# Selective scan on Trainium2: scan partitions regrouped from 128 channels to 8 channels x 16 states

## What is computed

```python
def step(h, inp):
    dt_t, B_t, C_t, u_t = inp
    dA = jnp.exp(dt_t[..., None] * A)
    dBu = (dt_t * u_t)[..., None] * B_t[:, None, :]
    h = dA * h + dBu
    y = jnp.einsum('bdn,bn->bd', h, C_t)
    return (h, y)
...
dt = jax.nn.softplus(jnp.einsum('blr,dr->bld', dt_lo, dt_w) + dt_b)
A = -jnp.exp(A_log)
y = _selective_scan(dt, Bm, Cm, xc, A, Dp)
y = y * jax.nn.silu(z)
```

## Time and profile before

| | |
|---|---|
| median of 3 runs | 5928.38 us (5915.49 to 5931.79) |
| the profiled execution: time, span | 5918.2 us, 5916.4 us |
| busy: PE, DVE, ACT | 81%, 89%, 58% |
| first scan starts, last scan starts | 66.0 us, 5722.6 us |
| mean granted TensorE clock | 0.883 of 2.4 GHz |
| DMA issues: b_rows and c_rows 256, bc_rows 64, patches 32, text 32, output 32, weights 14 | 430 |

### The profile page before, as it was taken

One profiled execution on the slowest core, in us unless ns is written; L12 is line 12 of the kernel. 1 busy time (PEld: TensorE's weight loads), 2 busy tenths in 40 slices (PEclk: granted clock), 3 DMA queues, 4 the chain that ended last, 5 costly groups with the idle time before them and its releaser, 6 DMA issues.

```text
span 5916.4 us, 67241 instructions
## 1 busy us (share of the span) xinstructions
PE 4785.9 (81%) x22624; PEld 3257.5 (55%) x22624; DVE 5259.6 (89%) x4154; ACT 3457.5 (58%) x7266; POOL 1.5 (0%) x9
## 2 busy tenths in 40 slices
PE   5788878877878787888788888888888888888877
PEld 3555555555555555555555555555555655555554
DVE  6999998989999898998999999898998989989971
ACT  3455655555565555665556666566565656656643
POOL 0000000000000000000000000000000000000000
PEclk8888988888889888888889999998999989989985
DMA  3112211212112112112112111112112112111110
GB/s 105 59 44 67 66 41 60 68 38 67 58 43 68 61 45 68 55 47 66 60 45 67 63 45 60 61 45 66 54 47 68 45 60 66 41 61 60 41 32 2
DMA packets 56890, 327.57 MB, mean 55 GB/s; under 512 B 13245, under 2 KB 15741, under 8 KB 23626
## 3 DMA queue, kind: packets, MB, share of 16 engines
q1 hardware_dynamic: 56490, 322.53, 17.3%
HBM read 313.52 MB, written 8.98 MB: 55 GB/s over the span
## 4 chain that ended last, share of the span: by engine, by line
DVE 42%; PE 37%; issue 16%; ACT 4%; DVEq 1%; DMA 0%; SPq 0%; ACTq 0%; POOL 0%; POOLq 0%
DVE hs L993 15%; PE y_ps L426 9%; DVE hs L997 7%; DVE hs L976 5%; PE f_ps L549 4%; DVE neg_max L1100 3%; PE f_ps L597 3%; PE f_ps L505 3%; DVE xc L1056 3%; PE f_ps L522 3%; PE f_ps L608 3%; PE f_ps L496 2%; PE a_ps L474 2%; PE f_ps L562 2%; PE a_ps L464 2%
## 5 line engine op out<-in xcount | busy, mean ns | idle before, releaser
L993 DVE TENSOR_TENSOR_SCAN hs<-decay,hs 128x2192 f32<-128x2192 f32 x384 | 1812.3, 4719 | 19.5 <-DVE decay L983 2.2
L426 PE MATMUL y_ps<-hs,ident 128*128 128x274 f32 x5376 | 1612.7, 433 | 81.9 <-DVE hs L1001 29.5
L736 ACT ACTIVATE decay<-dt,inner_s 128x273 f32<-128x273 f32 x3072 | 1384.7, 517 | 98.7 <-issue 53.1
L426 PEld LDWEIGHTS y_ps<-hs,ident 128*128 128x128 f32 x5376 | 1082.4, 208 | 445.5 <-issue 148.7
L976 DVE TENSOR_TENSOR hs<-b_rows,dtu 128x2192 f32<-128x2192 f32 x384 | 935.6, 2436 | 90.7 <-PE y_ps L426 67.7
L997 DVE TENSOR_TENSOR hs<-hs,c_rows 128x2192 f32<-128x2192 f32 x384 | 935.0, 2435 | 4.5
L549 PE MATMUL f_ps<-ident,hid 92*92 92x92 f32 x3456 | 481.8, 283 | 507.3 <-ACT hid L820 507.3
L549 PEld LDWEIGHTS f_ps<-ident,hid 92*92 92x92 f32 x3456 | 340.9, 141 | 694.1 <-ACT hid L820 616.3
L820 ACT ACTIVATE hid<-f_ps,neg_max 92x274 f32<-92x274 f32 x1152 | 463.3, 481 | 341.3 <-DVE neg_max L1100 341.1
L464 PE MATMUL a_ps<-xn,w_in_s 96*128 96x274 f32 x1536 | 472.9, 435 | 8.9 <-ACT xi L759 5.4
L1100 DVE TENSOR_REDUCE neg_max<-f_ps 92x4 f32<-92x1096 f32 x288 | 370.4, 1286 | 92.2 <-PE f_ps L542 92.0
(11 more groups left out here) (114 smaller groups left out, 5115.3 us busy)
## 6 DMA issues: line engine op xcount, KB each, us to landing
b_rows<-bc_rows SPq DMA_DIRECT2D x128, 1096.0 KB, 5.6
c_rows<-bc_rows SPq DMA_DIRECT2D x128, 1096.0 KB, 5.6
xp<-in_patches SPq DMA_DIRECT2D x32, 588.0 KB, 7.4
out<-h SPq DMA_DIRECT2D x32, 205.5 KB, 2.2
bc_rows<-bc_s SPq DMA_DIRECT2D x64, 34.2 KB, 1.5
h<-in_txt SPq DMA_DIRECT2D x32, 57.8 KB, 2.3
w_in_s<-in_w_in SPq DMA_DIRECT2D x1, 1152.0 KB
fc_s<-in_fc SPq DMA_DIRECT2D x2, 576.0 KB
```

The costliest lines, as they stand in the source:

```text
L426: mm = pe.matmul(y_ps[:, 0:T], ident[:, :], hs[q % 2][:, n, :], start=(q % 2 == 0 and n == 0), stop=(q % 2 == 1 and n == end - 1))
L736: e = act.activation(decay[half][:, n, t], dt[d][:, u, t], ACT.Exp, scale=inner_s[:, d, u, s:s + 1])
L993: dve.tensor_tensor_scan(i, a, i, 0.0, ALU.mult, ALU.add).then_inc(scan_done, 1)
```

## The change

The scan's partitions become 8 channels x 16 states, and its eight free tiles hold 64 channels, so a unit is again two scans of 128 x 2192.

- dt and dtu (dt * u) are written by channel to device memory (write_rows, 12 writes an element) and read back with each channel's row repeated for its 16 states, dt into decay and dtu into hs (read_half, 24 reads an element of 1.1 MB each). decay has three buffers, hs four. ACT takes the exponential in place. dt and dtu have one buffer each for both directions.
- B and C are one tile each for a direction. A matmul with a selection matrix spreads the 16 rows over the 128 partitions: B stays in PSUM (b_ps), C is copied to SBUF (c_s). spread_rows and its loads are gone.
- The state sum is eight matmuls a scan with 32 output columns each (y_pick), in four column groups; the paired additions are gone.
- a_ps is one bank, as b_ps takes the other: each matmul of the front waits for the copy of the one before.
- The softplus runs by chunk. Its max(x, 0) moves from DVE to ACT (Relu), and the zeroing of the edges too, now for every scan.
- x_proj and the step sizes move by one gap, and the output product, the scan and the next input product stand in the order of gaps 0, 1, 2. A set-up builds the selection matrices and A's columns once.

```diff
+        b_ps = ctx.enter_context(nc.psum_tensor("b_ps", [128, 512], F32))
+        a_ps = ctx.enter_context(nc.psum_tensor("a_ps", [128, 512], F32))
...
+        dt_rows = nc.dram_tensor("dt_rows", (2, IC, 32, 4, T), F32, kind="Internal").ap()
+        def row_of_channels(rows, d, u):
+            return rows[d, u].rearrange("r a t -> a r t")
+
+        def half_unit(rows, q):
+            halves = rows[q // 6, (q // 2) % IC].rearrange("(e h b) a t -> e h (b a t)", h=2, b=2)
+            return halves[:, q % 2, :].unsqueeze(1).broadcast_to([EDD, N, TILES * T])
...
+            def write_rows(b, d, u):
+                before = anew(ago(b, 1), SCANS, 6 * d + 2 * u + 2, 40 * b[1] + 30 + 3 * d + u)
+                sp.wait_ge(dt_ready, at(b, 6, 3 * d + u + 1))
+                wait(sp, exp_done, before)
+                sp.dma_start(row_of_channels(dt_rows, d, u), dt[:, u, :]).then_inc(dt_stored[u], 16)
+                sp.wait_ge(dtu_ready, at(b, 6, 3 * d + u + 1))
+                wait(sp, dbu_done, before)
+                sp.dma_start(row_of_channels(dtu_rows, d, u), dtu[:, u, :]).then_inc(dtu_stored[u], 16)
+
+            def read_half(b, q):
+                d, u = q // 6, (q // 2) % IC
+                sp.wait_ge(dt_stored[u], at(b, 32, 16 * (d + 1)))
+                wait(sp, scan_done, anew(b, SCANS, q - 2, 40 * b[1] + 2 * q + 1))
+                sp.dma_start(decay[q % 3][:, :, :], half_unit(dt_rows, q)).then_inc(dt_in[q % 3], 16)
+                sp.wait_ge(dtu_stored[u], at(b, 32, 16 * (d + 1)))
+                wait(sp, ysum, anew(b, SCANS, q - 3, 40 * b[1] + 2 * q + 2))
+                sp.dma_start(hs[q % 4][:, :, :], half_unit(dtu_rows, q)).then_inc(dtu_in[q % 4], 16)
+
+            def first_rows(b):
+                write_rows(b, 0, 0)
+                read_half(b, 0)
+                write_rows(b, 0, 1)
+                read_half(b, 1)
+                write_rows(b, 0, 2)
...
             def step(b, f, e, a):
                 if a is not None:
                     load_patches(a)
+                read_half(b, 2)
+                read_half(b, 3)
+                read_half(b, 4)
                 if e is not None:
                     store(e[0])
                 if a is not None:
                     load_txt(a)
-                spread_rows(b, 1)
+                read_half(b, 5)
+                write_rows(b, 1, 0)
+                read_half(b, 6)
+                write_rows(b, 1, 1)
+                read_half(b, 7)
+                write_rows(b, 1, 2)
+                for q in range(8, SCANS):
+                    read_half(b, q)
                 if a is not None:
-                    spread_rows(a, 0)
+                    first_rows(a)
...
+            def sum_states(b, q):
+                wait(pe, hc_done, at(b, SCANS, q + 1))
+                if q % 2 == 0:
+                    wait(pe, gate_tmp, at(b, UNITS, q // 2))
+                for v in range(2):
+                    for g in range(4):
+                        mm = pe.matmul(y_ps[32 * g:32 * g + 32, 0:T], y_pick[:, 2 * (q % 2) + v, :],
+                                       hs[q % 4][:, 4 * v + g, :], start=(q % 2 == 0 and v == 0),
+                                       stop=(q % 2 == 1 and v == 1), skip_group_check=True)
+                mm.then_inc(ysum, 1)
...
             def in_proj(b, d, lo, hi):
                 if lo == 0:
                     pe.wait_ge(xn_ready, at(b, 1, 1))
+                    wait(pe, c_copied, at(b, 2, d))
                 for j in range(lo, hi):
+                    if j >= 1:
+                        pe.wait_ge(xz_copied, at(b, 12, 6 * d + j))
...
+            def c_spread(b, d):
+                pe.wait_ge(dtv_abs, at(b, 6, 3 * d + 3))
+                pe.wait_ge(dtv_relu, at(b, 6, 3 * d + 3))
+                pe.matmul(a_ps[:, 0:T], spread[32:32 + 2 * N, 1, :], dt_lo[32:32 + 2 * N, :],
+                          start=True, stop=True).then_inc(c_mm, 1)
+
+            def b_spread(b, d):
+                pe.wait_ge(dtlo_ready, at(b, 2, d + 1))
+                wait(pe, dbu_done, at(b, SCANS, 6 * d))
+                pe.matmul(b_ps[:, 0:T], spread[32:32 + 2 * N, 0, :], dt_lo[32:32 + 2 * N, :],
+                          start=True, stop=True).then_inc(b_mm, 1)
...
             def exps(b, q, lo, hi):
...
+                    act.wait_ge(dt_in[q % 3], at(b, 64, 16 * (q // 3) + 16))
+                    t = 0 if d == 0 else T - 1
+                    act.activation(dec[:, :, t:t + 1], zero_c[:, 0:1].unsqueeze(1).broadcast_to([128, TILES, 1]),
+                                   ACT.Copy).then_inc(edge, 1)
+                for k in range(lo, hi):
+                    t = slice(1, T) if d == 0 else slice(0, T - 1)
+                    e = act.activation(dec[:, k, t], dec[:, k, t], ACT.Exp,
+                                       scale=a_cols[:, d * IC + u, TILES * half + k:TILES * half + k + 1])
...
+            def dt_parts(b, d, j):
                 act.wait_ge(dtv_mm, at(b, 6, 3 * d + j + 1))
+                wait(act, dtu_stored[j], at(b, 32, 16 * d))
+                act.activation(dtu[:, j, :], a_ps[:, 0:T], ACT.Abs).then_inc(dtv_abs, 1)
+                wait(act, dt_stored[j], at(b, 32, 16 * d))
+                act.activation(dt[:, j, :], a_ps[:, 0:T], ACT.Relu).then_inc(dtv_relu, 1)
+                act.wait_ge(dtv_abs, at(b, 6, 3 * d + j + 1))
+                act.activation(dtu[:, j, :], dtu[:, j, :], ACT.Exp, scale=-1.0).then_inc(sp_exp, 1)
+                act.wait_ge(sp_exp, at(b, 6, 3 * d + j + 1))
+                act.activation(dtu[:, j, :], dtu[:, j, :], ACT.Ln, bias=one_c[:, 0:1]).then_inc(sp_ln, 1)
...
+            def input_product(b, q):
+                d, x = q // 6, hs[q % 4]
+                dve.wait_ge(dtu_in[q % 4], at(b, 48, 16 * (q // 4) + 16))
+                dve.wait_ge(b_mm, at(b, 2, d + 1))
+                dve.tensor_tensor(x[:, :, :], x[:, :, :], b_ps[:, 0:T].unsqueeze(1).broadcast_to([128, TILES, T]),
+                                  ALU.mult).then_inc(dbu_done, 1)
...
+            def output_product(b, q):
+                d, x = q // 6, hs[q % 4]
+                dve.wait_ge(scan_done, at(b, SCANS, q + 1))
+                dve.wait_ge(c_copied, at(b, 2, d + 1))
+                dve.tensor_tensor(x[:, :, :], x[:, :, :], c_s[d][:, :].unsqueeze(1).broadcast_to([128, TILES, T]),
+                                  ALU.mult).then_inc(hc_done, 1)
```

More of the change, by code:

```diff
@@ L666, in fronts_early @@
                 x, xd = (b, 1) if d == 0 else (a, 0)
-                if x is not None and gap == 9:
+                if x is not None and gap == XP_GAP:
                     x_proj_mm(x, xd)
@@ L670, in fronts_early @@
                     dt_mm(x, xd, DT_GAPS.index(gap))
+                if x is not None and gap == C_GAP:
+                    c_spread(x, xd)
+                if x is not None and gap == B_GAP:
+                    b_spread(x, xd)
                 if d == 0 and a is not None:
@@ L702, in front @@
                 b = (0, 0)
+                for u in range(UNITS):
+                    pe.wait_ge(s_l, u + 1)
+                    mm = pe.matmul(f_ps[:, 0, COLS * u:COLS * (u + 1)], a_spread(u), col_mask,
+                                   start=True, stop=True)
+                mm.then_inc(s_lm, 1)
                 tok(b, (0, 1))
@@ L715, in finish @@
                         fine_late(*e, 2 * GAPS + gap)
[L716 to L718 removed]
+                    if gap == 1:
+                        sum_states(f[0], SCANS - 1)
                     fine_early(*f, gap)
@@ L947, in front @@
                 for j in range(IC):
-                    dt_abs(b, 0, j)
-                for part in range(2):
-                    softplus(b, 0, part)
-                act.wait_ge(a_neg, 1)
-                exps(b, 0, 0, NH)
+                    dt_parts(b, 0, j)
+                c_copy(b, 0)
+                act.wait_ge(s_ac, 1)
+                exps(b, 0, 0, TILES)
             def finish(f, e):
```

308 lines of the change are left out of this document (140 added, 168 removed).

## The result

The kernel after the change took 7365.3 us, the median of its runs (7301.9 to 7392.1), against 5930.1 (5915.5 to 5944.3) for the kernel before on the same chip: a ratio of 1.241, 95% interval 1.238 to 1.244. It is slower by 1435 us. The prediction said 5725 and a range of 5550 to 6250. The profiled execution took 7392.1 us, its span is 7390.3.

What follows compares the result with a forecast made beforehand. It took DVE's work plus its waits on PE and ACT as the bound. 5918.2 - 195 - 140 + 30 + 80 (transfers) + 20 = 5713 us, stated as 5725 by the median of runs; range 5550 to 6250.

Steps and rivals of the forecast that it cites:

- R: Time of one read of dt or dtu from device memory, taken as 5.6 us on 8 engines.
- The rival: Rival 1: transfers become the bound, deciding from 5.8 us a read, slower from 6.1; priced at 6050 us, chance 0.24.
- that formula: Transfer-bound time: 24 R + 12 x 2.3 + 3 us an element, times 31.9, plus 86 and 194 us.
- rivals 3 and 4: Reads spread over 16 engines, 5645 us, chance 0.09; state sum's column groups don't run side by side, 5865, chance 0.03.
- DVE's own work, -195: Halving adds, step-size maxima and edge memsets leave DVE, 215.7 us; softplus by chunk adds 20.5; net -195.
- The state sum, -140: On PE, 16 short passes a scan, 0.7 us instead of 3.1, save 140 of DVE's 180.6 us of waits.
- ACT's added work, +190 and hidden: Edge copies, Relu, split Exp and Ln add about 190 us, hidden in ACT's 42% free time except where DVE waits.
- One bank, +30: Front's matmuls share one PSUM bank, PE waits for ACT's copies, delaying row maxima and MLP's sums; +30 us.
- rival 2: PE's chains lengthen: clock and bank double the 256.7 us of waits; 5950 us, clock near 0.7, chance 0.12.
- the three waits of 256.7 us: DVE's waits on chains of PE and ACT: rstd 105.4, row maxima 92.0, MLP's sums 59.3 us.
- The front, +20: Before the first scan: one write, one read and 12 copies and parts in series; +20 us, 10 to 35.
- the prediction for sixteen engines: Rival 3: reads spread over 16 engines, the 80 us for transfers go; 5645 us, chance 0.09.

Runs made afterwards that it cites:

- e3: Changed kernel with reads on 16 engines, two buffers for the output tile h2 and each write of rows split in four: 5938.7 us, ratio 1.001.
- e7: e6 with the state sum as eight full-width identity matmuls a scan instead of column groups (output not the reference's): 6114.4 us, ratio 1.031.
- e6: e3 with two PSUM banks for the front again and B copied to SBUF by ACT: 5947.6 us, ratio 1.003.
- e9: e3 without ACT's clearing copies at the edge and its Relu (output incomplete): 6042.3 us, ratio 1.020.
- e5: Kernel before the change with only the front's single PSUM bank and the one-gap shift of x_proj and step sizes: 5989.8 us, ratio 1.010.
- e12: e3 with ACT copying chunk 0 of the input projection in gap 0, ahead of the gelus: 5840.4 us, ratio 0.984.
- e1: Changed kernel with the repeat of the states outermost in the reads' source, so reads get 16 engines: 6111.0 us, ratio 1.030.
- e8: e3 with each read bringing one tile of eight, 140 KB instead of 1.12 MB (data left out): 5891.5 us, ratio 0.996.

## Why the prediction was wrong

**The step that failed** is the length of a read, R. It was right that a read gets 8 engines: 9437 completion packets of 4 bytes stand in the trace after, which is 768 reads x 8, 384 writes x 4, 96 loads and stores of the elements x 16, 13 weights x 16, and 12 and 1 for the two parts of the step-size weights. It was wrong to take 5.6 us from "At the slow start 16 engines fetch the same 8.8 KB at 237 GB/s; eight engines, each on a row of its own, ask for only 212". That sentence holds device memory to be the only thing that engines share. They also share the way into SBUF. Alone, a read takes 9.7 to 10.2 us; inside the kernel the packets average 469 ns, 7.5 us a read, close to the 0.445 us and 7.1 that the prediction had worked out as the mean of the kernel before and set aside. The rival's point of decision, 5.8 us, was computed rightly, the 0.2 us of margin should have been read as no knowledge at all, and the rival's own sum said 6690 for R = 7.1; pricing it at 6050 and ending the range at 6250 cut off what the argument had produced. R = 7.5 in that formula gives (24 x 7.5 + 30.6) x 31.9 + 280 = 6998 us. The kernel without the store's wait took 6965; its own packets average 450 ns, R = 7.2, and the formula gives 6768, so it is good to some 200 us and its hit with 7.5 is luck. (The chances have a slip too: those of the forecast and rivals 3 and 4 sum to 0.64, and with "a little of 2" to more than the 0.63 given for faster.)

**The store.** The prediction asked for each moved or added transfer what stands behind it, and didn't ask it for the transfers that were there. A store issued behind reads in the same queue landed after 20.2 us instead of 2.2, with DVE waiting: 400 us in the kernel after, 129 with the reads on sixteen engines.

**DVE's own work, -195:** right. -200.9 in the kernel after (5259.6 to 5058.7), the input product from PSUM at 2429 ns.

**The state sum, -140:** right in kind, too low in size. The waits of 180.6 us went to 3.6 in the kernel after and to 30.7 in e3; full-width sums cost 167 us (e7 against e6). Sixteen passes load in 0.62 us at full clock, where 0.7 was said.

**ACT's added work, +190 and hidden:** right. The groups add up to 189 us (edge copies 81.5, Relu 75.3, splits 13.3 and 18.9), ACT's busy time rises only by 94.4, since neighbouring instructions overlap (their durations sum to 174 us more, the time with any of them running is 94 us more), and e9's undisturbed large elements are no shorter without 157 us of it.

**One bank, +30:** the mechanism was right, the size wrong, and of the two victims named the second, the MLP's sums, was hit in the changed kernel. In the kernel before it costs 57 us (e5) and hits a third, the state sum; in the changed one it costs at least 98, the part that e12 gives back. The prediction looked for slack ahead of the waits on average ("slack of two gaps lies ahead of most of them") and not for the one gap where ACT has 7 us of other work before its copy.

**Clock:** the granted mean fell from 0.883 to 0.724 of 2.4 GHz, near the 0.7 of rival 2, whose waits of over 400 us on PE and ACT are there too. They are in good part transfers' waits passed on: row maxima fall from 405.0 to 240.5 us in e1 and 225.3 in e3. But with the transfers mended rival 2 is nearly there: the three waits of 256.7 us, which the term of +30 let grow little and the rival let double, are 594.1 us in e3 and 471.4 in e12, +215. What the clock of 0.79 itself costs isn't isolated; e7 shows that more work on PE isn't the cure.

**The front, +20:** the first scan starts at 99.6 us instead of 66.0, +34, within the bounds of 10 to 35.

**What stays open.** e12 is at 5840, the prediction for sixteen engines was 5645. Of these 195 us the stalls at the loop's edge and the waits for rows come to some 33 to 47 by e8, the later first scan is some 25 (90.6 us against 66.0) and was told at 20. The rest is in the waits for row maxima (219.9 against 92.0), the MLP's product (116.0 against 59.3), rstd (135.5 against 105.4) and o_s (102.3 against 41.2), chains through PE and ACT at a lower clock and in another order of gaps; the runs don't split these.

## What to carry to other kernels

Before a transfer is given a rate, count its engines and then look at which partitions they write at the same moment; where the engines' blocks met, up to half the rate was lost, and a small load-only kernel showed it. Weigh it against the number of engines: the form that mended this kernel has the same slow packets on twice as many. When traffic triples, list every transfer that already shares the queue and who waits for it, not only the new ones. When a buffer goes from two to one, search the order of the engine that empties it for its longest piece of other work, and put the emptying first.

## What the hardware did that I had not expected

- With nothing else running, packets of 8768 bytes take mostly 331 ns or about 660, which fits whether another engine writes 32 partitions away at that moment: 114 GB/s on eight engines, 195 to 218 on sixteen, and 263 for the same bytes in the form of one row to 128 partitions.
- The queue's own issue blocks. An issue takes some 0.6 us; in the kernel after, behind reads and unsplit writes of rows, it took up to 15.18. Reads in flight alone don't do it: e3 has the same bytes in flight and no issue over 2 us.

```profile
2991.61 15.18 SPq L370 DMA_DIRECT2D xp<-in_patches  x1
3007.04 0.63 SPq L393 DMA_DIRECT2D decay<-dt_rows  x1
...
3113.88 14.49 SPq L393 DMA_DIRECT2D decay<-dt_rows  x1
```

- At the loop's edge ACT and PE stand for up to 8.4 us once or twice an iteration, with traffic, and for less than 3 with an eighth of it. Leaving out instructions made ACT's stalls longer by 46 us.
- Three times the bytes, dealt over all engines, cost little (e8 puts them at 33 to 47 us): e12 moves 949 MB where the kernel before moves 323, at 70.7% of the queue, and is faster.
